# A planned attention and expert kernel: TensorE's waits are put in front of an earlier item, and the plan gets other prices and shifts

## What is computed

```python
x = x + attention(layernorm(x))      # 16 heads of 16, causal softmax
x = x + ffn(layernorm(x))            # 8 experts, top 2 per token, and a shared pair
# attention: Q, K, V = x@Wq+bq, x@Wk+bk, x@Wv+bv
#   probs = softmax(causal(Q K^T / 4)), each key's column times a gate:
#   gate  = tanh(gelu(drift * g_w1 + g_b1) @ g_w2 + g_b2), drift from x @ dp_w1 by layernorm, gelu and dp_w2
#   out   = (probs * gate) @ V @ Wo + bo
# ffn: group-limited sigmoid router (4 groups of 2, 2 groups kept, 2 experts), weights * 2.5
#   y = sum_e weight_e * (silu(x w1_e) * (x w3_e)) w2_e  +  (silu(x sg) * (x su)) sd
```

## Time and profile before

| what | value |
|---|---|
| time, 3 runs | 1802.76 us median (1800.54 to 1803.23) |
| the profiled execution | 1808.59 us, of which the span from first to last instruction is 1806.6 us |
| TensorE busy | 1653.0 us, 91% of the span |
| DVE, ACT, POOL busy | 1292.4, 1081.9, 811.8 us |
| mean granted clock of TensorE | 0.962 |
| fillers (L858) | 135 |

### The profile page before, as it was taken

The page is one execution under the profiler, slowest core; times in us unless marked ns, Lnnn a source line. Parts: engine busy times, 40 slices in busy tenths (PEclk is TensorE's granted clock), DMA queues, the critical chain, the costliest instruction groups (busy, mean ns, idle before and its releaser), DMA issues.

```text
span 1806.6 us, 34673 instructions
## 1 busy us (share of the span) xinstructions
PE 1653.0 (91%) x12785; PEld 982.5 (54%) x12785; DVE 1292.4 (72%) x2528; ACT 1081.9 (60%) x1808; POOL 811.8 (45%) x1390
## 2 busy tenths in 40 slices
PE   7798989989988999899998989999999889999888
PEld 3344446435544566455654555555564557666677
DVE  5776767967795777777785757877688666963655
ACT  3466756665655655675656755586556765568432
POOL 5234533463345221632237863363207773157760
PEclk9699999999998999999998999999999999999999
DMA  5556655554445532644545665453535675336440
GB/s 151 158 156 194 176 169 152 182 153 124 125 127 147 158 104 87 174 113 120 159 118 151 185 194 152 127 162 108 147 93 172 198 197 159 97 129 199 135 122 13
DMA packets 192708, 261.25 MB, mean 145 GB/s; under 512 B 19616, under 2 KB 127264, under 8 KB 192544
## 3 DMA queue, kind: packets, MB, share of 16 engines
q1 hardware_dynamic: 181792, 229.67, 44.0%
q0 software_dynamic: 10752, 29.37, 5.6%
HBM read 130.98 MB, written 127.40 MB: 143 GB/s over the span
## 4 chain that ended last, share of the span: by engine, by line
PE 54%; DVE 14%; DMA 8%; ACT 8%; POOL 8%; issue 5%; SPq 3%; another core or an unknown queue 0%; POOLq 0%; ACTq 0%; DVEq 0%
PE ps_all L1961 10%; PE ps_all L2071 10%; DVE mx L1549 7%; PE ps_all L1941 6%; PE ps_all L1908 6%; PE ps_all L2102 5%; PE ps_all L1892 4%; ACT probs L1358 4%; PE ps_all L1878 3%; PE ps_all L1970 3%; POOL xs_s L1207 2%; PE ps_all L2081 2%; PE ps_all L2034 1%; DMA rr<-r_s 1%; DMA out<-rr 1%
## 5 line engine op out<-in xcount | busy, mean ns | idle before, releaser
L1549 DVE TENSOR_REDUCE mx<-ps_all 128x2 f32<-128x1024 f32 (+2 forms) x640 | 619.0, 1006 | 132.5 <-PE ps_all L1908 74.4
L1358 ACT ACTIVATE probs<-ps_all 128x1024 f32<-128x1024 f32 x576 | 571.8, 1028 | 218.0 <-PE ps_all L1941 209.9
L1175 POOL TENSOR_SCALAR_AFFINE_SELECT probs<-probs 128x256 f32<-128x256 f32 (+1 forms) x448 | 190.9, 443 | 495.5 <-ACT probs L1358 491.3
L1961 PE MATMUL ps_all<-probs,vaug 128*32 128x512 f32 (+3 forms) x3072 | 319.4, 516 | 21.9 <-POOL probs L1175 15.3
L1908 PE MATMUL ps_all<-k_st,q_st 63*128 63x512 f32 (+3 forms) x1536 | 269.3, 401 | 48.0 <-ACT probs L1358 16.3
L1941 PE MATMUL ps_all<-q_st,k_st 64*128 64x512 f32 (+3 forms) x1536 | 265.6, 401 | 29.3 <-ACT probs L1358 9.9
L1908 PEld LDWEIGHTS ps_all<-k_st,q_st 63*128 63x128 f32 x1536 | 135.1, 193 | 163.7 <-issue 52.2
L1941 PEld LDWEIGHTS ps_all<-q_st,k_st 64*128 64x128 f32 x1536 | 130.9, 191 | 158.9 <-issue 67.2
L2071 PE MATMUL ps_all<-w_hi,x2h 128*128 128x512 f32 (+1 forms) x480 | 168.2, 350 | 4.3 <-DVE x2l L1598 2.5
L1804 DVE SCALAR_TENSOR_TENSOR act_t<-act_t,ps_all 128x256 f32<-128x256 f32 x168 | 70.4, 419 | 123.4 <-ACT act_t L1421 110.9
L2071 PE MATMUL ps_all<-w_lo,x2h 128*128 128x512 f32 (+1 forms) x480 | 157.0, 327 | 0.0
(11 more groups left out here) (195 smaller groups left out, 2849.8 us busy)
## 6 DMA issues: line engine op xcount, KB each, us to landing
qk_s<-qh SPq DMA_DIRECT2D x116, 256.0 KB
q_st<-qk_s SPq DMA_DIRECT2D x128, 192.0 KB
k_st<-qk_s SPq DMA_DIRECT2D x128, 192.0 KB
xs<-xs_s SPq DMA_DIRECT2D x72, 256.0 KB
ys_s<-ysb SPq DMA_DIRECT2D x72, 256.0 KB
o_s<-o_sb SPq DMA_DIRECT2D x64, 256.0 KB
qk_s<-ql SPq DMA_DIRECT2D x57, 256.0 KB
xs_s<-ysb SPq DMA_DIRECT2D x20, 512.0 KB, 6.0
```

Of the source, the lines that this page charges most:

```text
L1175: last = nc.gpsimd.affine_select(out=block, in_=block, compare_op=ALU.is_ge, fill=0.0, base=0, pattern=[[0, heads], [1, P]], channel_multi ...
L1358: nc.scalar.activation(to, of, ACT.Exp, scale=DH ** -0.5).then_inc(freed[release[item][0]], 1)
L1549: last = nc.vector.tensor_reduce(to[:, :, p, qt % QPC], both[:, :, at:at + keys], X_AXIS, ALU.max)
L1961: last = mm(bank(first)[32 * h:32 * h + 32, q0 - c * CHUNK:], vaug[:, kt, g, h * VW:h * VW + 32], probs[:, s % 2, h, at:at + cols], start= ...
```

## The change

Three things change together.

1. While it writes TensorE's order, the plan now also notes which items were ready long before their turn. It keeps a *head*. If an item was ready (inputs and banks) at least `AHEAD` = 300 ns before the head's start, by the plan's time, its waits are issued with the head's, in front of the head's matmuls; otherwise it becomes the head itself. A `yield` between the waits and the matmuls of each of the functions makes that possible. 722 of the 2,503 items have their waits moved in this way, to 524 heads. Of the 722, 204 stand behind a `FULL` item and are `FULL`, 160 are `ROWS` behind `ROWS`, 15 `COLS` behind `COLS`, and 343 change the tiling. The two leading kinds of heads are `QK` (120) and `HT` (109); 29 heads are `MT`.
2. The plan's prices: `SWITCH` 100 to 130, `EXPOSED` 90 to 60, `SAME_TILING` 12000 to 7000. A change of tiling costs 130 in the plan, where it cost 190 (100 to `COLS`). An item without a change costs 60 more than its `ns` unless it is `PV` or `ED`, where it cost at most 90 more and only behind idle time.
3. The table `LATER` has 89 entries in place of 42, with larger numbers (up to 61000).

Counted over the whole of TensorE's order, changes of tiling go from 996 to 1134: into `ROWS` from 411 to 488, into `FULL` from 315 to 371, into `COLS` from 270 to 275. Fillers go from 135 to 70. Matmul instructions with at least one wait in front go from 2271 to 1740, those with two or more from 528 to 699, those with three or more from 50 to 264. The number of instructions of each kind on DVE, ACT, POOL and SP is unchanged.

```diff
+AHEAD = 300
-SWITCH, EXPOSED = 100, 90
+SWITCH, EXPOSED = 130, 60
-SAME_TILING = 12000
+SAME_TILING = 7000
...
-LATER = {"AC": 8000, "AQ": -1000, "AX": 7000, "CB": 6000, "CC": -41000, "CG": 3000, "CJ": 2000, "CL": -8000,
+LATER = {"AB": -3000, "AC": 25000, "AE": 16000, "AG": -27000, "AN": 2000, "AQ": -1000, "AR": 21000, "AS": 37000,
...
+        self.waits, self.release, self.start, self.idle, self.ahead = {}, {}, {}, {}, {}
+        head = None
...
                 if tile != tiling:
-                    ns += SWITCH + EXPOSED * (tile != COLS)
-                    tiling = tile
-                elif idle and tile != COLS:
-                    ns += min(EXPOSED, idle)
+                    ns, tiling = ns + SWITCH, tile
+                elif item[0] not in ("PV", "ED"):
+                    ns += EXPOSED
...
+                ready = max([ready] + [bank_at[b] for b in taken])
                 for b in taken:
                     bank_at[b] = None
+            if e == "PE":
+                if head and item[0] != "PX" and ready + AHEAD <= self.start[head]:
+                    self.ahead.setdefault(head, []).append(item)
+                else:
+                    head = item
...
             def turn_x(item, n, t):
                 pe.wait_ge(a_xn, n * TILES + t + 1)
                 own_banks(item)
+                yield
                 for k in range(KE):
...
+            heard_of = {}
+            for item in order["PE"]:
+                keep_busy(item)
+                work = heard_of.pop(item, None)
+                if work is None:
+                    work = steps[item[0]](item, *item[1:])
+                    next(work)
+                for later in plan.ahead.get(item, ()):
+                    heard_of[later] = steps[later[0]](later, *later[1:])
+                    next(heard_of[later])
+                for _ in work:
+                    pass
```

More of the change, by code:

```diff
@@ L247, in run @@
         uses, given = [[] for _ in range(BANKS)], [0] * BANKS
-        self.waits, self.release, self.start, self.idle = {}, {}, {}, {}
+        self.waits, self.release, self.start, self.idle, self.ahead = {}, {}, {}, {}, {}
+        head = None
         groups = {1: [[b] for b in range(BANKS)], 2: [[b, b + 1] for b in range(0, BANKS, 2)]}
@@ L279, in run @@
                         begin = max(begin, min(ready))
-                    found.append((max(begin, free_at[e]), due, tile, item))
+                    found.append((max(begin, free_at[e]), due, tile, item, begin))
                 if found:
@@ L287, in run @@
             cost = [f[1] + (SAME_TILING if f[2] and f[2] != tiling else 0) for f in found]
-            now, _, _, item = found[cost.index(min(cost))]
+            now, _, _, item, ready = found[cost.index(min(cost))]
             _, ns, _, _, banks, tile, frees, lands = self.items[item]
@@ L843, in all_work @@
             for item in order[name]:
-                if name == "PE":
-                    keep_busy(item)
                 steps[item[0]](item, *item[1:])
@@ L2105, in expert_down @@
                 last.then_inc(ed_full, 1)
[L2107 to L2109 removed]
+            steps = {"AT": turn_x, "AV": values, "AQ": queries_keys, "M": maximum, "MT": turn_max,
+                     "QK": scores, "PV": sums, "CW": project, "CT": turn_x2, "CG": logits, "CJ": turn_logits, "PX": place,
+                     "XT": turn_slots, "EU": expert_up, "HT": turn_h, "ED": expert_down}
+            heard_of = {}
[10 more added lines that the diff above has]
+                    pass
 def kernel(**inputs):
```

3 lines of the change are left out of this document (removed), and 16 rows, old and new, of the table LATER.

## The result

The changed kernel takes 1811.3 us in the median of 20 runs (1799.21 to 1819.82), the kernel before 1803.62 us in 20 runs beside them: a ratio of 1.0042 with a 95% interval of 1.0025 to 1.0060. One run of the kernel before took 1866.25 us, over 1.5% above its fastest, and the ratio goes by the others. The forecast was 1785, so the change went the other way, by 7.7 us. The profiled execution of the changed kernel has a span of 1810.3 us against 1806.6.

The account below looks back on a forecast made before the run. PE's own work was taken to bound over half the chain (54%), waits on others the rest. Terms 25.7 + 3.4 + 17 - 64 = -18 us on 1808.6 gave 1790.6, less 5.8 for the median: 1785; 8-in-10 range 1762 to 1827.

Parts of the forecast that it names:

- Step 1: PE's moved waits that were already fulfilled: moving them brings 0 us, at most 36 us if weight loads were freed.
- The rival of the freed weight loads: Moving waits lets PE's weight loads start earlier at 364 same-tiling items: 36 us more, 1749 us; chance 4%.
- Step 2: PE's added tiling changes (77 into ROWS, 56 into FULL, 5 into COLS) cost 25.7 us.
- Step 3: PE instructions with two or more waits grow by 171; a third really wait, 0.06 us each: 3.4 us.
- Step 4: Moved waits not yet fulfilled delay PE's heads: 40 late ones at 0.43 us, 17 us.
- hold back the heads: Rival: later items' waits delay the heads HT, QK and MT, making it slower, 1828 us; chance 22%.
- Step 5: The other order cuts PE's idle and filler time in the middle, as fillers fall 48%: -64 us.
- the idle time doesn't go: Rival: only a fifth of the middle's 111.9 us PE idle goes, and the clock loses 9: 1836 us; chance 13%.
- sign (5): Check in the changed profile: PE's middle idle time near 68 us; at 100 or more the forecast is wrong.

Follow-up runs that it names:

- moved_only: The kernel before in its own order, with 687 waits moved forward by the same rule: 0.9988 of the kernel before.
- more_changes: The kernel before with SAME_TILING at 4000 in place of 12000, giving 1135 tiling changes and 121 fillers: 1.0016 of the kernel before.
- known_waits: The kernel before, also waiting again for bank counts already waited for (two or more waits in 946 instructions, not 528): 1.0042 of the kernel before.
- own_waits: The changed kernel in the same order, no wait moved, 70 fillers: 1.0068 of the kernel before.
- own_70_pair: The same program as own_waits, measured again on one more chip beside own_137_pair: 1.0039 of the kernel before.
- twice_moved: The changed kernel with AHEAD at -600 in place of 300, so 1489 waits moved in place of 722: 1.0572 of the kernel before.
- prices_only: The changed kernel with the old LATER table and no wait moved (new prices kept; 1024 tiling changes, 99 fillers): 1.0063 of the kernel before.
- own_137: The changed kernel's order with no wait moved and 137 fillers in place of 70: 0.9973 of the kernel before.
- before_none: The kernel before in its own order without any filler: 1.0057 of the kernel before.
- before_74: The kernel before, order and waits untouched, with 74 fillers in place of 135: 1.0012 of the kernel before.
- before_227: The kernel before in its own order with 227 fillers in place of 135: 0.9988 of the kernel before.
- own_137_pair: The same program as own_137, measured again on another chip beside own_70_pair: 1.0033 of the kernel before.

## Why the prediction was wrong, by its steps

**Step 1, a fulfilled wait costs nothing: right.** At the boundary of `CG` and `EU` in the changed kernel, with the wait moved (440) and with its own (310), the load starts with the last matmul, as in the earlier trace rows:

```profile
440.56 0.28 PE L2014 MATMUL ps_all<-x2l,gw_hi 128*8 128x256 f32 x1
440.67 0.40 PE L2096 MATMUL ps_all<-w_hi,x2h 128*128 128x512 f32 x1
440.56 0.19 PEld L2096 LDWEIGHTS ps_all<-w_hi,x2h 128*128 128x128 f32 x1
...
310.17 0.28 PE L2014 MATMUL ps_all<-x2l,gw_hi 128*8 128x256 f32 x1
310.29 0.40 PE L2096 MATMUL ps_all<-w_hi,x2h 128*128 128x512 f32 x1
310.17 0.19 PEld L2096 LDWEIGHTS ps_all<-w_hi,x2h 128*128 128x128 f32 x1
```

The rival of the freed weight loads falls with it, and by moved_only, which gains at most 0.34% where 36 us would be 2%. The Trainium skill (TensorE: Matmul & The Clock Gate, Part 2, step 1) says that TensorE's queue pulls a weight load ahead of matmuls in flight; the two boundaries agree, with a fulfilled wait in between.

**Step 2, tiling changes: right, somewhat high.** Forecast 25.7 us, measured 20.2 in own time; more_changes has 19.9 for 139. The boundary of the earlier trace rows stands unchanged:

```profile
316.97 0.28 PE L2129 MATMUL ps_all<-w_hi,h_lo 128*128 128x256 f32 x1
317.18 0.50 PE L1958 MATMUL ps_all<-q_st,k_st 64*128 64x512 f32 x2
317.52 0.40 PE L1923 MATMUL ps_all<-k_st,q_st 63*128 63x512 f32 x2
```

317.68 - 317.25 = 0.43 with a change, 317.92 - 317.68 = 0.24 without.

**Step 3, several semaphores: right in kind.** known_waits shows that the price falls on real waits alone. It took every such wait to pay; only those do whose last release is waited for in front. They are some 150 in the changed kernel and some 140 before, so at 0.06 us the change pays under 1 us of it, where 3.4 stood.

**Step 4, unfulfilled moved waits, 17 us: too high, and no cause of the loss.** moved_only is at -0.12% with an interval that reaches +0.11%, the changed kernel at 1.0042 against 1.0068 and 1.0039 of its order with own waits. The waiting in front of `HT` did grow, from 8.0 to 19.2 us, of which 4.9 are there without moved waits (12.9 in own_waits), and that in front of `MT` from 9.2 to 15.0. The account's sum shows no loss by it: 239.0 us with moved waits, 235.7 in own_70_pair without. The rival built on this step ("hold back the heads") had the right sign and the wrong mechanism: no cost of it shows at a margin of 300, and at twice_moved's -600 it is 98 us.

**Step 5, less idle time, -64 us: this is the step that failed.** The waiting fell by 21 us, a third of that; 18 of the 21 are the fillers' own time, and outside of them it fell by 3, where 54 of PE's idle time were to go. It was sized by fillers, 135 to 70, which count what the plan foresees. That the plan foresees less is a fact about its prices first: prices_only foresees less too (99 fillers) and waits 5 us more than before, 16 more outside of fillers. How much of the changed order's missing saving is due to the prices and how much to the shifts stays open. The rival "the idle time doesn't go" named this mechanism and gave it 13%. In kind it is the one that came true, at -21 where it put -22; its 1836 was too high because it added 17 us for step 4 and 9 for the clock, and had 25.7 for step 2. The account's 20.2 + 4.3 - 21.2 is +3.3 for the profiled executions, and the medians have 7.7; the 4.4 between them aren't accounted for. In the sum itself the case's own range was added up wrong: with 54 of idle time and 28 for the fourth term it ends at 1806, not at 1798. Its sign (5) should have read 112 - 54 = 58 us, since of the 64 only 54 were idle time.

**What stood in no step** is that the kernel before was profiled in an execution whose PE signals come late in some 30 places. With them go 12.7 us of its time. Part of that stands in the earlier trace rows like any other idle time, and none of the orders that were run is without it. In the changed order, with own waits and 137 fillers, 22.7 us go with them, 10 more, and 10.9 us of waits for ACT's copy of the sums show where. The changed kernel has 12.5 us of these waits, against 1.7 in the kernel before. That is more than the 7.7 us of the result, but what the rest of the queue makes up for is not shown. The forecast took 48% off all idle time, late signals' included. Still, without late signals own_137 waits only 22 to 38 us less than before_none, before_74 and before_227 (220.4 against 242.0 to 258.4), so -64 didn't come there either.

**The clock.** The mean over the runs is 0.9593 in the changed kernel and 0.9655 in before (beside the first chip kernels). In step 5's rival I put it at 9 us; the account has 4.3. before_74 has the same fall (0.006) for 2.1 us, so fewer fillers may explain about a quarter of the 7.7 us; the interval of that 2.1 reaches from -1 to 5 us, and own_70_pair against own_137_pair shows nothing of it.

## What to carry to other kernels

A planner's forecast of idle time can't be used as a measure when the same change alters the planner's prices: take the waiting from traces, and let prices be those that the trace shows at item boundaries. An order in a tightly chained kernel is judged on more than one chip and hour: here one program came out at 0.9973 and at 1.0033 against the same kernel, and a variant measured at another hour had looked like a cure. Moving a wait forward is free while the awaited thing is surely there (moved_only, 0.9988), and dear when the margin is taken away (twice_moved, +5.7%).

## What the runs showed of the hardware that was not expected

PE's completion signals came 0.3 to 6 us late in some 30 places of an execution, or in almost none, whatever the kernel; for one order most of the places are the same from run to run (731, 941, 1156 and 1366 us in own_137_pair; 731, 939, 1156 and 1364 us in own_70_pair). The packets of the `instruction` queue q8, 105 in each, don't take longer with them (0.9 to 1.8 us in own_137_pair, 0.9 to 2.4 in own_137). The cause stays open.

A second semaphore to wait for costs nothing at a fulfilled wait. At a real one it costs 0.06 us if the wait in front of the load ends last, and nothing if the load's own does. Fillers raised the mean granted clock from 0.954 (none) over 0.963 (74) and 0.970 (135) to 0.973 (227); the ratios were 1.0057, 1.0012, 1 and 0.9988. Only the first step is clear of noise, and the 74 were measured on another chip than the rest.
